# Softmax denominators of the first attention: 256 queries a tile on TensorE, one pair of key tiles added on VectorE

## What is computed

```python
B, T, D = representations.shape          # 2, 1024, 128; 16 heads
cp = jax.nn.leaky_relu(jnp.einsum('btd,cd->btc', representations, Wc) + bc)
...
scores = jnp.einsum('bqhd,bkhd->bhqk', q, k) / SCALE
attn = jax.nn.softmax(scores, axis=-1)
out = jnp.einsum('bhqk,bkhd->bqhd', attn, v).reshape(B, T, V_DIM)
proj = jax.nn.leaky_relu(jnp.einsum('btv,dv->btd', out, Wo) + bo)
```

## Time and profile before

| | before |
|---|---|
| runs, us | 1066.05, 1068.36, 1081.1 (median 1068.36) |
| span of the profiled execution, us | 1003.7 |
| mean granted TensorE clock | 0.979 |
| PE busy in the span | 920.3 us, 92% |
| DVE | 764.0 us, 76% |
| POOL | 597.9 us, 60% |
| ACT | 538.3 us, 54% |
| first and last start of a denominator product | 177.6 and 613.7 us |

### The profile page before, as it was taken

How to read it: one execution, slowest core, us unless ns; L and a number is a source line. 1 busy time by engine, 2 the same in 40 slices (tenths; PEclk the granted TensorE clock), 3 DMA queues, 4 the chain that set the end, 5 groups by cost and what they waited for, 6 DMA issues and landing times. The chain is left out here.

```text
span 1003.7 us, 20954 instructions
## 1 busy us (share of the span) xinstructions
PE 920.3 (92%) x7704; PEld 489.4 (49%) x7713; DVE 764.0 (76%) x1332; ACT 538.3 (54%) x901; POOL 597.9 (60%) x533
## 2 busy tenths in 40 slices
PE   5799997999999999999989997899889787799997
PEld 3346563233333333333323233798788444488794
DVE  6978888888888889887888825883689998873514
ACT  1255345666766666666756775443266243274463
POOL 3660425788778777887777893123735886652333
PEclk9999998999999999999999999799999997999999
DMA  9372525111111101111101123567651200243462
GB/s 319 137 225 88 153 64 156 41 51 46 26 52 28 58 24 49 34 55 56 35 26 44 40 67 116 161 193 241 225 156 35 89 22 22 79 142 101 143 196 79
DMA packets 92308, 97.17 MB, mean 97 GB/s; under 512 B 23184, under 2 KB 68624, under 8 KB 91952
## 3 DMA queue, kind: packets, MB, share of 16 engines
q1 hardware_dynamic: 87088, 85.34, 27.8%
q0 software_dynamic: 5120, 10.50, 3.6%
HBM read 70.57 MB, written 24.77 MB: 95 GB/s over the span
## 5 line engine op out<-in xcount | busy, mean ns | idle before, releaser
L255 PE MATMUL ps<-ar 64*64 64x512 bf16 (+5 forms) x5312 | 538.6, 448 | 17.7 <-ACT ar L301 4.3
L255 PEld LDWEIGHTS ps<-ar 64*64 64x64 bf16 (+2 forms) x5312 | 268.5, 137 | 273.4 <-ACT ar L301 92.0
L277 DVE TENSOR_REDUCE small<-ps 128x2 f32<-128x1024 f32 (+2 forms) x276 | 307.2, 1140 | 52.0 <-PE ps L255 50.6
L301 ACT ACTIVATE ar<-ps 128x1024 f32<-128x1024 f32 (+1 forms) x304 | 285.4, 941 | 113.1 <-PE ps L255 106.5
L264 POOL TENSOR_TENSOR psum_sb<-psum_sb,ar 128x1024 f32<-128x1024 f32 x91 | 214.8, 2360 | 57.3 <-DVE on_sb L264 47.1
L264 POOL TENSOR_TENSOR ar<-ar 128x512 f32<-128x512 f32 (+1 forms) x80 | 79.2, 995 | 52.1 <-DVE ar L277 30.0
L323 POOL DMA_INDIRECT gT<-ysort,rt x48 | 46.9, 977 | 98.7 <-issue 97.7
L264 DVE TENSOR_TENSOR ar<-ps,ar 128x256 f32<-128x256 f32 (+4 forms) x56 | 56.2, 1011 | 47.9 <-PE ps L255 43.4
L264 POOL TENSOR_TENSOR psum_sb<-ar 128x1024 f32<-128x1024 f32 x32 | 75.9, 2372 | 16.8 <-ACT ar L301 15.6
L298 ACT COPY ar<-ps 128x256 f32<-128x256 f32 (+1 forms) x84 | 31.8, 386 | 80.8 <-PE ps L255 50.2
L255 PE MATMUL ps<-wA,xnT 128*128 128x512 f32 (+3 forms) x192 | 62.0, 447 | 5.3 <-DVE ar L264 2.7
(11 more groups left out here) (156 smaller groups left out, 1066.0 us busy)
## 6 DMA issues: line engine op xcount, KB each, us to landing
ar<-in_L_up SPq DMA_DIRECT2D x48, 384.0 KB, 4.1
ar<-in_L_b SPq DMA_DIRECT2D x32, 322.0 KB, 3.4
rec_sb<-lscr SPq DMA_DIRECT2D x64, 128.0 KB
scr<-ar SPq DMA_DIRECT2D x48, 128.0 KB, 2.1
ar<-xsort SPq DMA_DIRECT2D x40, 128.0 KB
ysort<-ar SPq DMA_DIRECT2D x40, 128.0 KB, 3.3
ar<-scr SPq DMA_DIRECT2D x32, 112.0 KB
xsort<-xs SPq DMA_DIRECT2D x12, 256.0 KB, 6.2
```

Of the source, the lines that this page charges most:

```text
L255: return self.e.matmul(o, l, r, start=start, stop=stop) if self.e else Nothing()
L277: return self.e.tensor_reduce(o, a, AX.X, op, negate=True) if negate else self.e.tensor_reduce(o, a, AX.X, op)
L301: return self.e.activation(o, a, fn, **kw) if self.e else Nothing()
```

## The change

TensorE's products for the denominators have 256 columns instead of 512, in four column groups of 32, one for each quarter of the two heads' 1024 columns, and all sources add up in the same place. In units 0 to 26 there are three sources, tile 7, GpSimd's sum (psum_sb, tiles 0 to 4 as before) and a new tile pair_sb (the name of ps2_sb here; the order prints ps_sb), in which VectorE adds tiles 5 and 6. In units 27 to 31 VectorE adds tiles 4 and 5 to pair_sb instead of adding tile 4 to GpSimd's sum; there are four sources. VectorE's addition stands behind the maxima of step 7 and waits for GpSimd's last addition of the same unit; GpSimd's first addition of the next unit waits for it. ScalarE copies 256 columns instead of 512 to lrow, one DMA instead of two lays them out, and VectorE's addition of two halves ahead of the reciprocal is gone.

```diff
-    lcol = sb("lcol", [128, 16])
+    lcol = sb("lcol", [128, 8])
@@ tensor
+        def summed(u):
+            pe.wait_ge(*at("exp", 8 * u + 7))
+            pe.wait_ge(*at("sums", u, 4 if u < BY_DVE else 3))
+            pe.wait_ge(*at("sums_dve", u))
+            chain = psum_sb[:, 1024 * (u % 2):1024 * (u % 2) + 1024]
+            own = range(7 if u < BY_DVE else 6, 8)
+            return [Ps[:, (8 * u + k) % NP, :] for k in own] + [chain, pair_sb]
...
-                pe.wait_ge(*at("exp", 8 * u + 7))
-                pe.wait_ge(*(at("sums", u, 4) if u < BY_DVE else at("sums_dve", u)))
-                for n, src in enumerate((Ps[:, (8 * u + 5) % NP, :],
-                                         psum_sb[:, 1024 * (u % 2):1024 * (u % 2) + 1024],
-                                         Ps[:, (8 * u + 6) % NP, :], Ps[:, (8 * u + 7) % NP, :])):
-                    for a in range(2):
-                        r = 64 * (n % 2) + 32 * a
-                        ins = pe.mm(ps[r:r + 32, b, :], onesf[:, 0:32], src[:, 512 * a:512 * a + 512],
-                                    start=n < 2, stop=n > 1)
+                sources = summed(u)
+                for n, src in enumerate(sources):
+                    for j in range(4):
+                        ins = pe.mm(ps[32 * j:32 * j + 32, b, 0:256], onesf[:, 0:32], src[:, 256 * j:256 * j + 256],
+                                    start=n == 0, stop=n == len(sources) - 1)
@@ vector, step 5'
-                dve.red(lsum, lcol[:, :].rearrange("p (a q) -> p q a", a=2), ALU.add).then_inc(*up(("lsum", u)))
-                dve.wait_ge(*at("lsum", u))
-                dve.rec(lsum, lsum).then_inc(*up(("lcol_dve", u)))
+                dve.rec(lsum, lcol[:, :]).then_inc(*up(("lcol_dve", u)))
@@ vector, steps
-                if i % 8 == 7 and i // 8 >= BY_DVE:
+                if i % 8 == 7:
                     u = i // 8
-                    a_ = psum_sb[:, 1024 * (u % 2):1024 * (u % 2) + 1024]
-                    dve.wait_ge(*at("exp", 8 * u + 4))
-                    dve.wait_ge(*at("sums", u, 3))
-                    dve.tt(a_, a_, Ps[:, (8 * u + 4) % NP, :], ALU.add).then_inc(*up(("sums_dve", u)))
+                    k = 5 if u < BY_DVE else 4
+                    dve.wait_ge(*at("exp", 8 * u + k + 1))
+                    dve.wait_ge(*at("sums", u, k - 1))
+                    if u >= 1:
+                        dve.wait_ge(*at("sum", u - 1))
+                    dve.tt(pair_sb, Ps[:, (8 * u + k) % NP, :], Ps[:, (8 * u + k + 1) % NP, :], ALU.add).then_inc(
+                        *up(("sums_dve", u)))
@@ scalar
-                act.acp(lrow[:, :], ps[:, bank["sum", u], :]).then_inc(*emptied(("sum", u), ("lrow", u)))
+                act.acp(lrow[:, 0:256], ps[:, bank["sum", u], 0:256]).then_inc(*emptied(("sum", u), ("lrow", u)))
...
-                    act.wait_ge(*(at("sum", u) if k > 4 else at("sums_dve", u) if k == 4 and u >= BY_DVE else
-                                  at("sums", u, max(k, 1))))
+                    alone = 5 if u < BY_DVE else 4
+                    act.wait_ge(*(at("sums", u, max(k, 1)) if k < alone else at("sums_dve", u) if k < alone + 2 else
+                                  at("sum", u)))
@@ gpsimd, the first addition of a unit
+                    if u >= 1:
+                        pool.wait_ge(*at("sums_dve", u - 1))
@@ sync
-                    sp.wait_ge(*at("lsum", u - 1))
-                sp.dma(lcol[:, 0:8], lrow[0:64:32, :]).then_inc(*landed(("lcol_in",)))
-                sp.dma(lcol[:, 8:16], lrow[64:128:32, :]).then_inc(*landed(("lcol_in", u)))
+                    sp.wait_ge(*at("lcol_dve", u - 1))
+                sp.dma(lcol[:, :], lrow[0:128:32, 0:256]).then_inc(*landed(("lcol_in", u)))
```

More of the change, by code:

```diff
@@ L520, in _program @@
     ps2_sb = sb("ps2_sb", [128, 1024])
+    pair_sb = ps2_sb[:, :]
     lrow = sb("lrow", [128, 512])
-    lcol = sb("lcol", [128, 16])
+    lcol = sb("lcol", [128, 8])
     mT = sb("mT", [48, 2 * 128], BF16)
```

## The result

| | before | after |
|---|---|---|
| median of the runs, us | 1074.03 (4 runs, 1066.05 to 1081.1) | 1113.96 (4 runs, 1112.63 to 1115.41) |
| ratio | | **1.036**, 95% interval 1.032 to 1.041 |
| span of a profiled execution, us | 1003.7 and, taken again beside the experiments, 1076.8 | 1113.8 |
| denominators of unit 0 to those of unit 27, us | 386.4 and 388.6 | 426.2 |

The kernel became slower by 3.6%, about 39 us; the forecast was +30. As ratios to 1068.4 the forecast was 1.028 and its range 1.010 to 1.043.

What follows compares the result with a forecast made beforehand. TensorE was taken to bound the kernel before; afterwards a ring of waits through GpSimd, VectorE and TensorE adds 1.15 us a unit. 31.0 - 0.5 - 0.5 = +30 us takes 1068.4 to 1098.4 us, range 1079 to 1114.

Steps and rivals of the forecast that it cites:

- The ring: VectorE's addition waits for GpSimd, delaying maxima, TensorE, on_sb and GpSimd's next additions: 14.86 us a unit against 13.71.
- TensorE's products: Denominators: six rounds 0.215 us apart instead of four of 0.43, 0.43 us less a unit, 11.6 in 27 units.
- The rival with loads of 110 ns that show: TensorE's denominators: weight loads not hidden, adding 17.8 us, 1116; part of the dearer case, chance 0.10 above 1110.
- The sum's size: Whole kernel: +31.0 us in 27 units, less 0.5 and 0.5, giving +30 us.
- the one on disturbed units: Units 0 to 26: 10 of 16.2 us delays covered, 10.6 us GpSimd side work added, leaving nothing.
- two terms of -0.5: Subtracted from 31.0: some 0.5 us for shorter copy and DMA behind the last unit; the other is not spelled out.
- the upper rival: "It is dearer": weight loads show (1116) or the clock falls in long waits (1107); above 1110, chance 0.10.
- It doesn't wait: VectorE's addition: GpSimd done before the last maxima, so no ring closes; 1058, up to 1068, chance 0.09.
- The disturbances are covered: Disturbed units: the ring has slack that side work fills; 1080 to 1090, most likely 1085, chance 0.18.
- signs (2) to (5): New profile: VectorE idles before the addition, TensorE before the projection, GpSimd's additions follow on_sb, TensorE's busy share falls.
- (2): VectorE idle ahead of the addition in most units, released by GpSimd's psum_sb, 0.8 to 1.5 us each.
- (5): TensorE's busy share between units 0 and 27 down from 98% to about 88%.

Runs made afterwards that it cites:

- e3: Changed kernel, VectorE's addition in units 0 to 26 cut to 16 of 1024 columns, same place and waits, TensorE taking tile 5 instead of the pair: 1.006.
- e4: Changed kernel, but in units 0 to 26 GpSimd adds only tiles 0 to 3, VectorE tiles 4 and 5, TensorE sums four sources: 1.012.
- e5: Changed kernel with a fourth source in units 0 to 26 (tile 7 summed twice), eight rounds instead of six: 1.045.
- e2: Changed kernel with VectorE's addition of the pair moved behind the maxima of step 0', waits and work the same: 0.998.
- e6: Changed kernel with seven pieces of GpSimd's side work moved from between its additions to behind the last addition of their unit: 1.036.
- e0: Kernel before, unchanged, profiled again under the conditions of these runs: 1.002, units 388.6 us.
- e9: Same kernel as e2, measured a second time: 0.9965, units 384.3 us.
- e1: Kernel before with only the new product shape: 256 columns, four sources, one DMA, no addition of halves, no pair added by VectorE: 0.9994.

## Why the prediction was right

**The ring**, the step on which everything rests, came as it was put together from rows. Forecast turn 14.76 (odd) and 14.96 (even) us, measured 14.75 and 14.85. Its pieces: three GpSimd additions 7.45 (measured 384.69 to 392.14: 7.45), GpSimd's end to the addition 0.11 (0.09), addition to denominators 3.30 (377.48 to 380.78: 3.30), denominators to on_sb's end 3.90 (380.78 to 384.69: 3.91). Unit 27 of the kernel before already did what all units do now, and reading it was worth more than any duration. The only piece off is the small reduction in even units, 0.1 instead of 0.2.

**That both terms stand in a row** is confirmed by taking each away: 1.0 us a unit without the addition's work (e3), 27 us in all without the wait (e4), 11.4 us back with TensorE's saving undone (e5), everything by the addition's place (e2). With TensorE's rounds kept at eight the steps from the kernel before to the changed one are +10.3 us for the addition that doesn't wait (e4), +38.6 for GpSimd's lateness (e5 less e4) and -11.4 for two rounds fewer (e5 less the changed kernel), 37.5 together.

**TensorE's products**: rounds of 0.215 us, loads hidden. The rival with loads of 110 ns that show would have had rounds 0.325 apart; it is out, and with it the rule of the Trainium skill ("TensorE: Matmul & The Clock Gate", Part 3) that a load overlaps a running matmul only in another row group, which for these loads the trace again does not bear out.

**The sum's size**: quiet units make 27 x (14.80 - 13.71) = 29.4 us, against 31.0 forecast. The units differ by 37.6. The step that was mis-sized is the one on disturbed units, which I let cancel: they cost 8.2 us more. Of the two terms of -0.5 in the sum one was the shorter way behind the last unit; the other stands for 10 covered and 10.6 added, which is +0.6, and no row gives it. Here is unit 9, first VectorE's wait for GpSimd:

```profile
346.40 1.23 DVE L264 TENSOR_TENSOR ps_sb<-ar 128x1024 f32<-128x1024 f32 x1 [2.98 <-POOL psum_sb L264]
```

TensorE behind it:

```profile
348.82 1.94 PE L255 MATMUL ps<-on_sb,wA 128*32 128x512 f32 x8 [3.05 <-DVE small L277]
```

With a gather between its additions GpSimd is 2 us later still, TensorE idles 3.05 us, and behind that the projection takes 1.94 instead of 1.07 us: the granted clock fell to 1.2 GHz there, with a mean of 0.57 from 348 to 352 us (unit 9 lasted 17.85 us against 14.43). In the units the granted clock averaged 0.98 instead of 1.00; it was lowest in unit 17:

```profile
455.00:477.00 22.00, 18.82 (x190) 6.45 (x190) 19.06 (x27) 9.42 (x11) 16.05 (x16) 0.84 0.11 34
```

Unit 17 lasted 19.70 us in this profile, and 15.38 in e6, where no such stretch fell into it. I had put the clock into the upper rival; it belonged into the sum. In the units the changed kernel's profile has six stretches at 1.2 GHz (units 9, 22, 25 and 27, and two in unit 17), that of e0 one. At the 1.65 us of e2 and e9 the five more would be 8.3 us, an estimate and an upper one, since not all of such a stretch falls where TensorE sets the pace. Side work on the ring has a price of its own: e3 waits in the same way and has no such stretch, and its disturbed units cost 3.3 us more than before (394.3 less 27 x 13.80, against 388.6 less 27 x 13.71). The two together are more than the 8.2, so how these divide stays open. The stretches also fell differently in e5 and e6, and in e2 and e9, which are one program, so some of it is chance of one execution.

**The rivals.** "It doesn't wait" was refuted by VectorE's 26.4 us of idle time ahead of the addition. Its price can't be read from e4 directly, which measured 1.012, about 1081, against my 1058 to 1068: e4 has eight rounds where the rival has six. With 0.43 us less its quiet units would be 13.16 and 13.74, 0.30 and 0.22 below the kernel before. That is an estimate, since no run has six rounds and this place without the wait; it is somewhat less than the 0.37 that I took from unit 27. "The disturbances are covered" was wrong in sign: they grew. The signs (2) to (5) came, (2) with 0.9 us in odd quiet units and 1.6 in even ones, a little over the 1.5 named, and (5) with a busy share of 87%, forecast 88.

**What was wrong beside the sum**: that 64.7 us lie outside the span. In the second profile it is 1.8 us (1078.6 less 1076.8). It changed nothing in the difference, since the sum used differences within the attention only, but a span that stands far below the runs' times should have warned that the profiled execution did not run like the timed ones.

## What to carry to other kernels

A wait costs what is queued behind the waiting instruction, not what waits for its result: here the denominators could spare the time, but the maxima behind the addition held a PSUM slot, and one place further down in the order the same addition costs nothing that shows. When work moves to an engine that another engine feeds, walk from the waiting instruction to the next time the feeding engine starts; if the walk comes back to it, every duration on the way counts, even of engines that idle. Look for a place in the old trace where the new pattern already runs, such as the units at the end of a loop, and read the price there.

## What the runs showed of the hardware

Matmuls of 256 float32 columns in four column groups of 32, each with its own weight load of 110 ns, start a round every 0.215 us at 2.4 GHz, half of the 0.43 of 512 columns: splitting a product into twice as many half as long ones costs TensorE nothing that shows (e1: 0.9994). A wait of 3.05 us on TensorE was followed by a stretch at 1.2 GHz; those of 1.13 and 1.91 us in the quiet units of the same profile were not. But the same program had such a stretch in unit 3 in e9 and none in e2, and it cost 1.65 us. A multiplication of 128x512 on VectorE that started 0.24 us behind a GpSimd addition took 2.67 instead of 0.68 us and ended 0.55 us after it (e2). The same kernel's parts around the attention took 568.6 us of span in its first profile (177.6 and 391.0) and 638.3 in its second (209.8 and 428.5), with nearly the same attention (386.4 and 388.6).
